# Self-attention probabilities of a fused decoder layer: rows in two 2-byte parts transposed by DMA, in place of 4-byte blocks flipped by TensorE

## What is computed

```python
x = x + self_attn(layernorm(x))         # one head of width 256
x = x + cross_attn(layernorm(x), ctx)   # four heads of width 64
x = x + ffn(layernorm(x))               # four experts, one for each token
# self_attn(h):
norm = ||h||;  s = h / norm
q = s @ Wq.T + bq;  v = s @ Wv.T + bv
probs = softmax(q @ (q @ A).T / sqrt(256))
return (probs @ v) * norm
```

## Time and profile before

| | us |
|---|---|
| median of 3 runs | 821.49 (821.43 to 824.14) |
| profiled execution | 824.94 |
| its span | 823.0 |
| TensorE busy in the span | 760.4 |
| VectorE busy | 629.1 |
| ScalarE busy | 457.3 |

### The profile page before, as it was taken

How to read it: one execution, slowest core, us unless ns; L and a number is a source line. 1 busy time by engine, 2 the same in 40 slices (tenths; PEclk the granted TensorE clock), 3 DMA queues, 4 the chain that set the end, 5 groups by cost and what they waited for, 6 DMA issues and landing times. The chain is left out here.

```text
span 823.0 us, 19881 instructions
## 1 busy us (share of the span) xinstructions
PE 760.4 (92%) x6226; PEld 686.0 (83%) x6227; DVE 629.1 (76%) x1608; ACT 457.3 (56%) x930; POOL 165.5 (20%) x254
## 2 busy tenths in 40 slices
PE   3878889999999999999999999999997768999996
PEld 2768779899898898988988889899895657999996
DVE  4983746797898888888889888888886754777773
ACT  2554536666766667666666666666664612444342
POOL 3100121212303123031230312303212011222221
PEclk9999989999999999999999999999999959999999
DMA  6233233213233131231312314213189290111110
GB/s 218 72 106 108 64 131 121 102 33 109 61 112 106 38 111 62 97 106 38 123 61 85 106 38 131 76 62 106 39 288 368 88 335 27 37 41 39 39 33 15
DMA packets 51146, 80.94 MB, mean 98 GB/s; under 512 B 4894, under 2 KB 29216, under 8 KB 50976
## 3 DMA queue, kind: packets, MB, share of 16 engines
q1 hardware_dynamic: 49232, 75.63, 27.2%
...
## 5 line engine op out<-in xcount | busy, mean ns | idle before, releaser
L1135 ACT ACTIVATE ps_cross<-flip 128x512 f16<-128x512 f32 (+1 forms) x256 | 124.8, 515 | 110.4 <-PE flip L847 89.3
L1360 DVE TENSOR_TENSOR ps_cross<-flip,ps_cross 128x512 f16<-128x512 f32 (+1 forms) x256 | 145.0, 584 | 29.4 <-ACT ps_cross L1135 28.5
L1321 ACT ACTIVATE exp_cross<-exp_cross,xneg 128x1024 f32<-128x1024 f32 (+1 forms) x128 | 122.7, 960 | 28.0 <-DVE xneg L1520 28.0
L847 PE MATMUL flip<-ident,exp_cross 128*128 128x128 f32 (+1 forms) x832 | 130.9, 280 | 6.7 <-DVE ps_cross L1360 3.6
L836 PE MATMUL scores<-keys_cross,qt 128*128 128x402 f32 x512 | 126.8, 369 | 4.9 <-DVE xneg L1520 3.1
L847 PEld LDWEIGHTS flip<-ident,exp_cross 128*128 128x128 f32 (+1 forms) x832 | 95.2, 142 | 14.2 <-DVE ps_cross L1360 5.1
L724 PE MATMUL scores<-keys_self,u_tile 128*128 128x512 f32 x384 | 102.2, 403 | 4.3 <-issue 2.4
L823 PE MATMUL flip<-vals_self,ps_self 128*128 128x256 f32 x768 | 104.1, 290 | 0.0
L858 PE MATMUL cross_out<-vals_cross,ps_cross 128*128 128x128 f16 (+1 forms) x832 | 100.6, 222 | 0.2 <-DVE ps_cross L1360 0.2
L823 PEld LDWEIGHTS flip<-vals_self,ps_self 128*128 128x128 f32 x768 | 97.2, 195 | 0.0
L860 PE MATMUL cross_out<-vals_cross,ps_cross 128*128 128x64 f16 (+1 forms) x832 | 94.0, 194 | 0.0
...
## 6 DMA issues: line engine op xcount, KB each, us to landing
...
w_piece<-W SPq DMA_DIRECT2D x32, 256.0 KB, 2.9
w_dram<-w_high SPq DMA_DIRECT2D x32, 256.0 KB, 2.3
w_dram<-w_piece SPq DMA_DIRECT2D x32, 256.0 KB, 2.7
...
u_tile<-u_dram SPq DMA_DIRECT2D x16, 256.0 KB, 2.7
```

The source lines that it names most:

```text
L847: tr = pe.transpose(flip[0:rows, bank(use), n * P:(n + 1) * P], exp_cross[:, h % 2, m * P:m * P + rows], ident[:, :])
L1135: return act.activation(out, in_, ACT.Copy, **kw)
L1321: act.activation(exp_cross[:, h % 2, cols], exp_cross[:, h % 2, cols], ACT.Exp, bias=xneg[:, h % 2, 1:2], scale=-1.0, accum_out=xden[:, ha ...
L1360: return dve.tensor_tensor(out, full, hi, ALU.subtract)
```

## The change

- The self values are kept as two 2-byte parts, scaled so that they fit: the prologue computes a bound on the values' magnitude from the weights and the bias (a sum of squares, a product with ones on TensorE, a root on GpSimd, some small operations on VectorE), and `norms` takes the scale back out. ScalarE's copy of the values gets the scale, and VectorE's low part becomes a `scalar_tensor_tensor`.
- `exp_self` [128 x 2048, 4-byte] is split into a high and a low 2-byte row while it is still in rows, in two halves of 1024 columns: ScalarE copies `exp_self` times 16384 into `self_p[:, 0]`, VectorE subtracts into `self_p[:, 1]`. `self_flip` and `ps_self` are gone.
- SP issues four transposing DMAs a tile (two halves, high and low, 128 x 1024 elements of 2 bytes each) from `self_p` to `self_turn`, behind the load of `u_tile` and ahead of `keep_piece`.
- TensorE's self values read `self_turn`; groups 0 and 1 stand behind the output projection `wo`, groups 2 and 3 behind the first cross values of head 0. Some cross steps move with them.
- VectorE makes the low parts of head 0's groups 1 and 2 ahead of x1.
- The bias rows of the last stage are loaded behind the last part of `w2s`.

The diff, cut to what sets the order; left out are the declarations, the waits of the prologue on TensorE and GpSimd, and `norms`' scaling:

```diff
@@ -508,6 +518,17 @@
                 sp.wait_ge(scores_ready, 4 * j + 4)
                 loads_a(j + 1)
             if k < T:
+                for half in range(2):
+                    at = slice(half * N // 2, (half + 1) * N // 2)
+                    to = slice(half * T // 2, (half + 1) * T // 2)
+                    sp.wait_ge(self_p_hi, 2 * j + half + 1)
+                    if k >= 1:
+                        sp.wait_ge(self_p_used, 4 * j)
+                    sp.dma_start_transpose(out=self_turn[:, 0, to, :], in_=self_p[:, 0, at]).wait_op(
+                        constants_set, CONSTANTS, "sem-ge").then_inc(self_turned[half], 16)
+                    sp.wait_ge(self_p_lo, 2 * j + half + 1)
+                    sp.dma_start_transpose(out=self_turn[:, 1, to, :], in_=self_p[:, 1, at]).wait_op(
+                        constants_set, CONSTANTS, "sem-ge").then_inc(self_turned[half], 16)
                 sp.wait_ge(piece_hi, j + 1)
                 sp.wait_ge(piece_lo, j + 1)
...
@@ -547,13 +568,13 @@
         sp.wait_ge(x1_ready, T)
         load_w1(2)
         load_w1(3)
-        sp.dma_start(b1_row[:, :], bass.AP(io["b1"].tensor, 0, [[0, P], [1, E * DF]])).then_inc(b_loaded, 16)
-        sp.dma_start(b2_row[:, :], bass.AP(io["b2"].tensor, 0, [[0, P], [1, E * D]])).then_inc(b_loaded, 16)
         sp.wait_ge(cross_scores_ready, 8 * T)
         for e in range(E - 1):
             load_w2(e)
         sp.wait_ge(cross_p_used, 16 * T)
         load_w2(E - 1)
+        sp.dma_start(b1_row[:, :], bass.AP(io["b1"].tensor, 0, [[0, P], [1, E * DF]])).then_inc(b_loaded, 16)
+        sp.dma_start(b2_row[:, :], bass.AP(io["b2"].tensor, 0, [[0, P], [1, E * D]])).then_inc(b_loaded, 16)
         sp.wait_ge(spare_stored, 16 * E)
         sp.wait_ge(pads_out, 16 * (T + 1))
...
@@ -806,21 +835,13 @@
             three(scores[:, n, :], lambda a, c: u_tile[:, a * C + c, :],
                   lambda b, c: keys_self[:, b, c, n * 512:(n + 1) * 512]).then_inc(scores_ready, 1)
-        def self_flip(j, k, g):
-            use = ("s", g)
+        def self_values(j, k, g):
             if g % 2 == 0:
-                pe.wait_ge(self_exp, 2 * j + g // 2 + 1)
-            for n in range(4):
-                m = 4 * g + n
-                tr = pe.transpose(flip[:, bank(use), n * P:(n + 1) * P], exp_self[:, m * P:(m + 1) * P], ident[:, :])
-            tr.then_inc(self_flipped, 1)
-
-        def self_values(j, k, g):
-            pe.wait_ge(self_p_lo, 4 * j + g + 1)
+                pe.wait_ge(self_turned[g // 2], 32 * (j + 1))
             for n in range(4):
                 m = 4 * g + n
                 for a, b in ((0, 0), (0, 1), (1, 0)):
-                    mm = pe.matmul(self_out[:, 0:D], ps_self[:, g % 3, a, n * P:(n + 1) * P], vals_self[:, m, b, :],
+                    mm = pe.matmul(self_out[:, 0:D], self_turn[:, a, m, :], vals_self[:, m, b, :],
                                    start=(m == 0 and a == 0 and b == 0), stop=(m == T - 1 and a == 1))
             mm.then_inc(self_p_used, 1)
...
@@ -946,67 +967,43 @@
                 cross_values(j, k, 3, 0)
             if b:
                 cross_scores(j, k, 0, 0)
-            if a:
-
-                if k == 1:
-                    pe.wait_ge(self_p_lo, 4 * j)
-                elif k > 0:
-                    pe.wait_ge(cross_p_lo, 16 * j - 19)
-                self_flip(j, k, 0)
             if c:
                 cross_values(j, k, 3, 1)
                 pe.wait_ge(cross_p_lo, 16 * j - 18)
                 cross_flip(j, k, 3, 3)
+            if b:
+                cross_scores(j, k, 0, 1)
+            if c:
+                cross_values(j, k, 3, 2)
+            if b:
+                cross_scores(j, k, 1, 0)
+            if c:
+                cross_values(j, k, 3, 3)
+            if b:
+                cross_scores(j, k, 1, 1)
+            if c:
+                pe.wait_ge(cross_p_lo, 16 * j - 16)
+                small(("o",), j, k, o_ready, j - 1, o_flipped, flip_row(o_tile[:, :, :].rearrange("p h d -> p (h d)")))
+            if b:
+                if k > 1:
+                    pe.wait_ge(cross_p_lo, 16 * j - 19)
+                cross_flip(j, k, 0, 0)
+            if c:
+                pe.wait_ge(ot_lo, j - 1)
+                small(("wo",), j, k, ot_lo, j - 1, wo_ready,
+                      lambda out: three(out[:, 0:D], lambda a, c: ot[:, a, c, :], lambda b, c: wo_cross[:, b, c, :]))
             if a:
                 if k == 1:
                     pe.wait_ge(qt_ready, j)
                 elif k > 0:
                     pe.wait_ge(cross_p_lo, 16 * j - 17)
-                self_flip(j, k, 1)
-            if b:
-                cross_scores(j, k, 0, 1)
-            if c:
-                cross_values(j, k, 3, 2)
-            if a:
-
-                pe.wait_ge(self_p_lo, 4 * j + 1)
-                self_flip(j, k, 2)
-            if b:
-                cross_scores(j, k, 1, 0)
-            if c:
-                cross_values(j, k, 3, 3)
-            if a:
-
-                pe.wait_ge(self_p_lo, 4 * j + 2)
                 self_values(j, k, 0)
-
-                pe.wait_ge(self_p_lo, 4 * j + 3)
-                self_flip(j, k, 3)
-            if b:
-                cross_scores(j, k, 1, 1)
-            if c:
-
-                pe.wait_ge(cross_p_lo, 16 * j - 16)
-                small(("o",), j, k, o_ready, j - 1, o_flipped, flip_row(o_tile[:, :, :].rearrange("p h d -> p (h d)")))
-            if a:
                 self_values(j, k, 1)
-            if b:
-
-                if k == T:
-                    pe.wait_ge(cross_p_lo, 16 * j - 19)
-                else:
-                    pe.wait_ge(self_p_lo, 4 * j + 4)
-                cross_flip(j, k, 0, 0)
-            if c:
-
-                pe.wait_ge(ot_lo, j - 1)
-                small(("wo",), j, k, ot_lo, j - 1, wo_ready,
-                      lambda out: three(out[:, 0:D], lambda a, c: ot[:, a, c, :], lambda b, c: wo_cross[:, b, c, :]))
-            if a:
-                self_values(j, k, 2)
-                self_values(j, k, 3)
             if b:
                 if k > 1:
...
@@ -1016,14 +1013,18 @@
                 pe.wait_ge(cross_p_lo, 16 * j - 15)
                 cross_flip(j, k, 0, 2)
                 cross_values(j, k, 0, 0)
+            if a:
+                self_values(j, k, 2)
+                self_values(j, k, 3)
+            if b:
+                cross_scores(j, k, 2, 0)
+                cross_values(j, k, 0, 1)
                 if k == T:
                     pe.wait_ge(cross_p_lo, 16 * j - 17)
                 else:
                     pe.wait_ge(x1_ready, j + 1)
                 cross_flip(j, k, 0, 3)
-                cross_scores(j, k, 2, 0)
-                cross_values(j, k, 0, 1)
                 pe.wait_ge(cross_p_lo, 16 * j - 14)
                 cross_flip(j, k, 1, 0)
...
@@ -1166,7 +1167,9 @@
                 xt_hi_pro(g + 1)
             for n in range(4):
                 act.wait_ge(pro_v_biased, 4 * g + n + 1)
-                copy(vals_self[:, 4 * g + n, 0, :], v_tmp[:, n % 2, :]).then_inc(pro_v_hi, 1)
+                act.wait_ge(self_scale_step, 2)
+                act.activation(vals_self[:, 4 * g + n, 0, :], v_tmp[:, n % 2, :], ACT.Copy,
+                               scale=self_scale[:, 0:1]).then_inc(pro_v_hi, 1)
             u_hi(g)
             if g == 0:
...
@@ -1217,13 +1220,12 @@
                 act.wait_ge(cross_p_used, 16 * t + 4 * h + g - 3)
             copy(ps_cross[0:rows, g, 0, 0:w], flip[0:rows, bank(use), 0:w]).then_inc(cross_p_hi, 1)
-        def self_hi(j, k, g):
-            act.wait_ge(self_flipped, 4 * j + g + 1)
-            if g == 3:
-                act.wait_ge(self_p_used, 4 * j + 1)
-            elif k >= 1:
-                act.wait_ge(self_p_used, 4 * j if g == 0 else 4 * j + g - 3)
-            copy(ps_self[:, g % 3, 0, :], flip[:, bank(("s", g)), :]).then_inc(self_p_hi, 1)
+        def self_hi(j, k, half):
+            at = slice(half * N // 2, (half + 1) * N // 2)
+            act.wait_ge(self_exp, 2 * j + half + 1)
+            if k >= 1:
+                act.wait_ge(self_turned[half], 32 * j)
+            copy(self_p[:, 0, at], exp_self[:, at], scale=P_TOP).then_inc(self_p_hi, 1)
         def body(j, k):
             a, b, c = k < T, 1 <= k <= T, k >= 2
...
@@ -1264,11 +1266,8 @@
                 act.activation(barrier[:, 1:2], ident[:, 0:1], ACT.Gelu).then_inc(gelu_table, 1)
             if a:
                 self_hi(j, k, 1)
-                self_hi(j, k, 2)
             if b:
                 cross_exp(j, k, 0, 0)
-            if a:
-                self_hi(j, k, 3)
             if c:
                 act.wait_ge(o_flipped, j - 1)
                 copy(ot[:, 0, :, :], flip[:, bank(("o",)), 0:D].rearrange("p (c s) -> p c s", c=C)).then_inc(ot_hi, 1)
...
@@ -1304,7 +1303,7 @@
             if half == 0:
                 act.wait_ge(self_max, j + 1)
                 if k >= 1:
-                    act.wait_ge(self_p_used, 4 * j)
```

(33 more changed lines are left out.)

53 lines of the change are left out of this document (39 added, 14 removed).

## The result

The changed kernel takes 896.66 us (median of four runs, 896.18 to 898.04); the kernel before, run beside it, 822.81 us. The ratio is 1.089, with a 95% interval of 1.087 to 1.092. The direction was forecast, the size was not: the forecast was 861 us and the range ended at 890.

A forecast was written before the change was run, and what follows sets the result against it. VectorE's queue bounds the tile ahead of the projection, TensorE's work behind it. Loop +36.4, prologue +2.5, end +1 sum to +39.9 us, giving 861 us; own range 846 to 874, cut at 815 and 890.

The forecast's parts named there:

- The walk: Loop, one tile followed on three engines: projection at 20.2 us, 16.4 behind it, tile 36.6 against 33.9, +2.6 us.
- TensorE's three waits: Loop, ahead of the projection: for the second cross maximum, the output and its low half, some 4.6 us a tile.
- The low half of 1024 columns: VectorE in the loop: two from SBUF replace four of 512 columns, 1.15 each, 2.3 us for 2.4.
- a landing: Transposing DMAs in the loop: 2.9 us each, one behind another, the fourth ends at 25.0, cost nothing.
- Rival 1: Loop: TensorE's work decides, so the tile takes 31.9 us and the kernel 795 us; chance 0.19.
- rival 2: Loop: slow transposes become the bound; 3.5 us each gives 897 us, blocks one after another about 940; chance 0.12.
- The Trainium skill's rule: Transposing DMAs: such transfers run as fast as regular ones, so the sum stays as it is.
- rival 3: Loop: TensorE's clock falls with its waits, 2.5 us a tile, +35, 896 us; chance 0.05.
- the sign: Loop: a granted clock under 0.95 would show that TensorE's clock falls.
- The prologue: Ahead of the loop: VectorE's added work for the bound on the values, +2.5 us, ends 0.5 and 4.
- Tiles 0 and 1: First tiles: uncovered transposes against four rounds of flip, eviction and low half gone; nothing, ends -3 and +6.
- the end: Last stage: first instruction waits for bias rows moved behind the last weights, +1 us, ends 0 and 4.

The follow-up runs named there:

- experiment 1: The changed kernel with useless flips of the identity on TensorE that fit into its waits; 876.26 us, ratio to before 1.062.
- Experiments 2: The changed kernel with VectorE's and ScalarE's order changed, self low halves later, head 3's last low part ahead of them; 868.04 us.
- 4: The changed kernel with only the high halves transposed and VectorE's two self low halves left out too; 841.0 us.
- 5: The kernel before with 2-byte self probabilities and values, constant scale 4096, its own flips and order; 821.58 us, ratio 0.9965.
- 3: The changed kernel with only the high halves transposed, two DMAs a tile left out, all self-value products reading the high part; 895.14 us.
- experiment 7: The changed kernel with a constant scale of 4096 for the self values, the computed bound left out; 896.76 us.
- experiment 8: The changed kernel with the bias loads behind the last stage's first row loads, waited for at the first bias addition; 895.86 us.
- experiment 6: The changed kernel with self values group 0 ahead of the output's flip and group 1 ahead of the projection; 885.22 us.

## Why the prediction was wrong

*What held.* The walk. TensorE's three waits, their releasers and their order are those that the trace of the changed kernel shows; ahead of the projection they and three short ones come to 3.8 us in the tile shown, for the 4.6 forecast. The low half of 1024 columns takes 1.22 us (1.15 to 1.20 was taken), ScalarE's copy 1.08 (1.05), a landing 2.7 us (2.9), a 2-byte self value 0.110 us from start to start (0.114). At full clock (experiment 1) the tile is 36.85 us for a forecast of 36.5, and behind the projection 16.25 for 16.4. Experiments 2 and 4 show that VectorE's queue sets when the projection starts, 5 that the 2-byte operations themselves cost nothing, 3 that the transposes don't either in this order. Rival 1 fell: the projection came no earlier. So did rival 2: four transposes, 32 blocks of 128x128, are issued and landed between 433.61 and about 440.8, in 7 us. The prediction's estimate from the figure of the Trainium skill for one block (VectorE: DVE Perf Modes, section The three transpose paths), one block after another, would have made that 42; so the blocks do not follow one another like that. The Trainium skill's rule that such transfers are as fast as others (Advanced Engine Details and Errata, section X-Bar Transpose (TRN2)) fits the trace: 2.7 us to landing beside 2.4 to 2.9 for plain transfers of the same size.

*The step that failed* is rival 3, the clock. The mechanism was written down with its place and its price of 2.5 us a tile, but as an alternative with a chance of 0.05, dismissed because "the waits come in pieces of under 2 us". In the sum the clock stands at nothing. It is no alternative to the forecast: it follows from it, since each tile of the forecast has 4.6 us of waits close together. The pieces were indeed under 2 us, and that did not help: the trace has waits of 1.54 and 1.36 us within four microseconds and the lower level right behind them, in every tile of the loop, a granted clock of 0.93 where the prediction named under 0.95 as the sign. It costs 1.55 us a tile, 20 of the 31.5 us by which the forecast change of the span (39.9) fell short of the measured one (71.4). That the rival's own time, 896 us, is the measured one is partly luck: the time at the lower level was what it took, about 5 us a tile (0.93 granted over 38.4 us), but it cost 1.55 and not 2.5, and the terms below made up for it.

*Terms mis-sized.* The walk, +2.9 for +2.6 a tile (4.3 us in 13 periods): the first self low half waited 0.43 us for ScalarE, as forecast, but a gap of 0.19 ahead of the second maximum came on top (it is there in experiment 1 too; the one of 0.35 ahead of `xt` is not, and so goes with the clock). The prologue, +5.0 for +2.5 in this profile, past its upper end of 4; but over the profiles with the same prologue the middle one gives 106.30 - 102.50 = 3.8, inside the ends, of which the bound is some 3 (experiment 7). Tiles 0 and 1, +0.7 for nothing. The part from tile 15 on, +7.5 for 3.6 (a tile of 2.6 and 1 for the end): the wait for the biases is 3.1 (7.57 - 4.43; experiment 8 shows that it is theirs), the rest is tile 15's share of clock and walk. Together 20.2 + 4.3 + 2.5 + 0.7 + 3.9 = 31.6 us, what was missing. The first two, of the loop, are firm; the other three are read from one pair of profiles, and such pieces outside the loop differ by 1 to 4 us between profiles in which nothing there was changed. One more slip, without weight: the forecast's own range ends at 874, but its terms at their upper ends (prologue +1.5, tiles 0 and 1 +6, end +3) give 861 + 10.5 = 871.5.

*What stays open*: why the part from tile 15 on took back what experiment 7 gained, why the clock falls for longer in some tiles than in others, and whether the moved work could be placed without the loss (the order named in experiment 6).
